# The first layer of a two-layer graph attention kernel: adjacency in four column quadrants, weights turned in 32x32 blocks on VectorE, and masks and low halves on GpSimd

## The reference

```
h = relu(layernorm(x))
Wh1, Wh2 = (h @ W) @ a[:256], (h @ W) @ a[256:]
e = leaky_relu(Wh1 + Wh2.T, 0.2)
attention = softmax(where(adj > 0, e, -1e12), axis=1)
negative  = -softmax(where(adj > 0, -e, -1e12), axis=1)
x = x + elu(concatenate([attention @ h, negative @ h], axis=1) @ wtrans)
```

## Time and profile before

| | |
|---|---|
| median of 3 runs | 2782.67 us (2781.08 to 2784.18) |
| profiled execution, its own time | 2782.04 us |
| its span | 2780.3 us |
| first block, first instruction of l0b to first of g0 | 69.2 to 1099.9 us |
| PE busy | 2666.2 us, 96% |
| DVE busy | 2351.9 us, 85% |
| ACT busy | 1558.1 us, 56% |
| POOL busy | 1216.3 us, 44% |

### The profile page before, as it was taken

The page is one execution under the profiler, slowest core; times in us unless marked ns, Lnnn a source line. Parts: engine busy times, 40 slices in busy tenths (PEclk is TensorE's granted clock), DMA queues, the critical chain, the costliest instruction groups (busy, mean ns, idle before and its releaser), DMA issues. The chain is left out here.

```text
span 2780.3 us, 54929 instructions
## 1 busy us (share of the span) xinstructions
PE 2666.2 (96%) x20240; PEld 2550.2 (92%) x20240; DVE 2351.9 (85%) x3292; ACT 1558.1 (56%) x2419; POOL 1216.3 (44%) x706
## 2 busy tenths in 40 slices
PE   4799999999999997999999999997999999999997
PEld 2699999999999996899999999997899999999997
DVE  8898998888888894488888988888588888988888
ACT  5466666666666664555555555554455555555554
POOL 5444444544555440044444444445044454544446
PEclk8899999999999999999999999999999999999999
DMA  2222222222222221133333333333233333333333
GB/s 102 78 77 79 68 79 77 81 69 75 75 76 79 73 63 54 52 88 103 92 107 92 107 94 103 94 96 101 97 88 111 96 114 96 114 96 102 107 97 109
DMA packets 100926, 247.53 MB, mean 89 GB/s; under 512 B 9360, under 2 KB 51088, under 8 KB 100752
## 3 DMA queue, kind: packets, MB, share of 16 engines
q1 hardware_dynamic: 98880, 243.30, 29.5%
q10 hardware_dynamic: 1872, 1.84, 0.2%
HBM read 232.52 MB, written 12.58 MB: 88 GB/s over the span
## 5 line engine op out<-in xcount | busy, mean ns | idle before, releaser
L91 PE MATMUL l0b_acc<-l_h_parts,l0b_turned_hi 128*128 128x512 f32 x1984 | 759.0, 415 | 0.0
L485 POOL TENSOR_SCALAR l_adj_pieces<-l_adj_pieces 128x1024 f32<-128x1024 f32 x124 | 471.1, 3799 | 502.4 <-DMA l_adj_pieces<-in_adj_dram 502.4
L92 PE MATMUL l0b_acc<-l_h_parts,l0b_turned_lo 128*128 128x256 f32 x1984 | 556.4, 280 | 0.0
L503 ACT CAST l0b_turned_hi<-l0b_turn_psum 128x512 fp32r<-128x512 f32 x512 | 299.5, 586 | 336.2 <-PE l0b_turn_psum L668 332.1
L1066 POOL TENSOR_TENSOR g0b_sum_wide<-g0b_sum_wide,g0b_slab 128x512 f32<-128x512 f32 x240 | 311.4, 1298 | 396.2 <-DVE g0b_masked_psum L1174 386.1
L1066 POOL TENSOR_TENSOR g1b_sum_wide<-g1b_sum_wide,g1b_slab 128x512 f32<-128x512 f32 x240 | 316.0, 1317 | 339.2 <-DVE g1b_masked_psum L1174 328.4
L589 DVE TENSOR_TENSOR l0b_turned_lo<-l0b_turn_psum,l0b_turned_hi 128x512 fp32r<-128x512 f32 x512 | 351.8, 687 | 120.8 <-ACT l0b_turned_hi L503 118.2
L91 PEld LDWEIGHTS l0b_acc<-l_h_parts,l0b_turned_hi 128*128 128x128 f32 x1984 | 374.1, 189 | 66.3 <-issue 0.3
L92 PEld LDWEIGHTS l0b_acc<-l_h_parts,l0b_turned_lo 128*128 128x128 f32 x1984 | 374.9, 189 | 0.0
L80 PE MATMUL g0b_acc<-g_wh_parts,g0b_part_hi 128*128 128x256 f32 x1024 | 293.6, 287 | 6.8 <-DVE g0b_part_lo L1180 5.7
L80 PE MATMUL g1b_acc<-g_wh_parts,g1b_part_hi 128*128 128x256 f32 x1024 | 293.6, 287 | 5.7 <-DVE g1b_part_lo L1180 4.6
(11 more groups left out here) (219 smaller groups left out, 7317.0 us busy)
## 6 DMA issues: line engine op xcount, KB each, us to landing
g_adj_ring<-in_adj_blocks_dram SPq DMA_DIRECT2D x256, 512.0 KB, 3.7
l_adj_pieces<-in_adj_dram SPq DMA_DIRECT2D x128, 512.0 KB, 3.8
l0b_x_in<-in_x_dram SPq DMA_DIRECT2D x32, 128.0 KB, 3.1
x_rows<-l0b_x SPq DMA_DIRECT2D x32, 128.0 KB, 3.0
g0a_rows<-x_rows SPq DMA_DIRECT2D x8, 512.0 KB, 4.7
g0b_y<-x_rows SPq DMA_DIRECT2D x16, 256.0 KB, 4.1
v_rows<-g0b_y SPq DMA_DIRECT2D x16, 256.0 KB, 4.5
g1a_rows<-v_rows SPq DMA_DIRECT2D x8, 512.0 KB, 5.2
```

The lines of the kernel that those rows point to most:

```text
L91: pe.matmul(out, lhs_hi, rhs, start=first, stop=False)
L92: return pe.matmul(out[:, width:], lhs_lo, rhs[:, :width], start=False, stop=False)
L485: pool.tensor_scalar(adj_pieces[:, q, :], adj_pieces[:, q, :], 0.0, PENALTY, ALU.is_le, ALU.mult).then_inc(penalty_ready, 1)
L503: act.copy(turned_hi[:, s % RING, :], turn_psum[:, s % RING, :]).then_inc(hi_ready, 1)
```

## The change

Another layout of adj, another engine for four of the operations, and another order of work.

- The host cuts adj into blocks of 32 rows, and each into column quadrants: block f is a [128, 1024] tile whose partition (q, r) holds row r of the block, and of every 128 columns the 32 of quadrant q. A tile of 128 rows is four such blocks a. `r_quad` and `s_quad` hold r and s in that layout, both divided by 2^60; ACT writes the former in four small pieces per group in l0a, and l0a ends with a spread of s over the quadrants (four small matmuls) and some small tables (`own`, `fold`).
- Penalties are adj - 1 on POOL, a `tensor_tensor` subtract of a broadcast 1.0 (L535), in place of `tensor_scalar` (L251 and L485). l0a makes none.
- The score is one ACT instruction, Prelu with bias s, from `r_quad` to PSUM (L559), in place of DVE's L567. The masked scores are still DVE's, with the factor 2^60 in them (L632), and now read the score from PSUM.
- In this layout turning the 32 x 32 blocks where they stand gives the turned weights, so that DVE's `transpose` of 1024 columns, SBUF to SBUF (L657), takes the place of the 64 TensorE turns per tile. It reads four row blocks at once, so it waits for four exponentials of its sign.
- `split` on ACT (L574) now works on 1024 columns from SBUF. `rest`, the low half, moves from DVE and PSUM to POOL and SBUF (L541), 8 per tile with 1024 columns.
- A row's maximum and sum now lie in four partitions: `turn_max`, `join_max`, `spread_max`, `take_max` for the maximum and `spread_sum`, `totals` for the sum join them through small TensorE and DVE operations.
- The order is one list of steps n, unrolled, eight to a tile: masks at n, exponentials 9 steps behind, turns 13, split and rest 14, weighing 16. The rings hold three entries, and the score two.

The diff's core (the counterparts of `mean_rows`, `project_means` and elu only change their indices):

```diff
-                    for q in range(PIECES):
-                        pool.wait_ge(adj_in[q], 16)
-                        pool.tensor_scalar(adj_pieces[:, q, :], adj_pieces[:, q, :], 0.0, PENALTY,
-                                           ALU.is_le, ALU.mult).then_inc(penalty_ready, 1)
...
                     def take_r(g):
                         act.wait_ge(r_ready, g + 1)
-                        act.copy(r_row[:, g * BANK:(g + 1) * BANK], r_psum[:, g % 2, :]).then_inc(r_copied, 1)
+                        by_quad = r_psum[:, g % 2, :].rearrange("p (b q c) -> p q b c", q=4, c=QUAD)
+                        for q in range(4):
+                            here = slice(q * QUAD, (q + 1) * QUAD)
+                            last = act.mul(r_quad[here, g * P:(g + 1) * P].rearrange("p (b c) -> p b c", c=QUAD),
+                                           by_quad[here, q, :, :], 1.0 / FAR)
+                        last.then_inc(r_copied, 1)
...
+                    for a in range(4):
+                        last = pe.matmul(s_psum[:, a * T:(a + 1) * T], spots[:, a, :, :].rearrange("p q r -> p (q r)"),
+                                         s_high[:], start=True, stop=True)
+                    last.then_inc(s_spread, 1)
...
+            POS_RING, NEG_RING = 2, 3
+            TURN_RING = 3
+            PART_RING = 3
+            SLOTS = 8
+            FRONTS = T * SLOTS
+            TO_EXP, TO_TURN, TO_SPLIT, TO_WEIGH = SLOTS + 1, SLOTS + 5, SLOTS + 6, 2 * SLOTS
...
+                    for n in range(STEPS):
+                        f, rest = divmod(n - 1, 2)
+                        if rest == 0 and 0 <= f and f + ADJ_SLOTS < T * 4:
+                            sp.wait_ge(masked, 2 * f + 2)
+                            fetch_adj(sp, f + ADJ_SLOTS)
...
-                    with pool.Fori(32, 16 * T + 16, 16) as arrived:
-                        for q in range(PIECES):
-                            pool.wait_ge(adj_in[q], 16)
-                            pool.wait_ge(adj_in[q], arrived)
-                            pool.tensor_scalar(adj_pieces[:, q, :], adj_pieces[:, q, :], 0.0, PENALTY,
-                                               ALU.is_le, ALU.mult).then_inc(penalty_ready, 1)
+                    def penalty(f):
+                        slot = adj_ring[:, f % ADJ_SLOTS, :]
+                        pool.wait_ge(adj_in[f % ADJ_SLOTS], 16 * (f // ADJ_SLOTS + 1))
+                        pool.tensor_tensor(slot, slot, unit[:].to_broadcast([P, PIECE]), ALU.subtract
+                                           ).then_inc(penalty_ready, 1)
+
+                    def rest(m):
+                        pool.wait_ge(hi_ready, m + 1)
+                        wait(pool, products, m - PART_RING + 1)
+                        pool.tensor_tensor(turned_lo[:, m % PART_RING, :, :], turned[:, m % TURN_RING, :, :],
+                                           turned_hi[:, m % PART_RING, :, :].bitcast(F32), ALU.subtract
+                                           ).then_inc(lo_ready, 1)
+
+                    pool.memset(max_parts[:], 0.0).then_inc(padded, 1)
+                    penalty(0)
+                    for n in range(STEPS):
+                        f, odd = divmod(n, 2)
+                        if odd == 0 and f + 1 < T * 4:
+                            penalty(f + 1)
+                        if 0 <= n - TO_SPLIT < FRONTS:
+                            rest(n - TO_SPLIT)
...
+                    def score(f):
+                        t, a = divmod(f, 4)
+                        wait(act, masked, 2 * (f - 1))
+                        act.activation(score_psum[:, f % 2, :], r_quad[:], ACT.Prelu, bias=s_quad[:, a, t:t + 1],
+                                       alpha=SLOPE_0).then_inc(score_ready, 1)
...
+                    def split(m):
+                        act.wait_ge(turns, m + 1)
+                        wait(act, products, m - PART_RING + 1)
+                        act.copy(turned_hi[:, m % PART_RING, :, :], turned[:, m % TURN_RING, :, :]
+                                 ).then_inc(hi_ready, 1)
...
+                    for n in range(STEPS):
+                        if 0 <= n - TO_SPLIT < FRONTS:
+                            split(n - TO_SPLIT)
+                        if 0 <= n - TO_EXP < FRONTS:
+                            exponential(n - TO_EXP)
+                        f, odd = divmod(n, 2)
+                        if odd == 0 and f + 1 < T * 4:
+                            score(f + 1)
...
-                            dve.scalar_tensor_tensor(
-                                out=score[:], in0=r_row[:, cols], scalar=s_high[:, bass.ds(t, 1)],
-                                in1=r_row_low[:, cols], op0=ALU.add, op1=ALU.max).then_inc(score_ready, 1)
...
-                        n = G2 * t + s
-                        dve.wait_ge(hi_ready, n + 1)
-                        dve.tensor_tensor(turned_lo[:, s % RING, :], turn_psum[:, s % RING, :],
-                                          turned_hi[:, s % RING, :].bitcast(F32), ALU.subtract
-                                          ).then_inc(lo_ready, 1)
...
+                        t, a, sign = front(f)
+                        tau = 4 * t + a
+                        dve.wait_ge(score_ready, tau + 1)
+                        dve.wait_ge(penalty_ready, tau + 1)
+                        if f == 0:
+                            dve.wait_ge(padded, 1)
+                        if a == 0 and sign == 0:
+                            wait(dve, max_turned, t - 1)
+                        ring = POS_RING if sign == 0 else NEG_RING
+                        if t >= ring:
+                            dve.wait_ge(turns, SLOTS * (t - ring) + 4 * (sign + 1))
+                        dve.tensor_tensor_reduce(part(t, sign)[:, a, :], adj_ring[:, tau % ADJ_SLOTS, :],
+                                                 score_psum[:, tau % 2, :], FAR, LOWEST,
+                                                 ALU.add if sign == 0 else ALU.subtract, ALU.max,
+                                                 max_parts[:, t % 2, 2 * a + sign:2 * a + sign + 1]
+                                                 ).then_inc(masked, 1)
...
+                    def join_max(t):
+
+                        dve.wait_ge(max_turned, t + 1)
+                        wait(dve, max_spread, t)
+                        folded = max_psum.rearrange("p (o q r) -> p o r q", o=1, r=QUAD)
+                        dve.tensor_reduce(max_joined[:], folded.to_broadcast([P, 4, QUAD, 4]), AX, ALU.max,
+                                          negate=True).then_inc(max_join, 1)
...
+                    def take_max(t):
+                        dve.wait_ge(max_spread, t + 1)
+                        wait(dve, exp_ready, SLOTS * (t - 1))
+                        dve.tensor_copy(neg_max[:, t % 2, :, :].rearrange("p a s -> p (a s)"), spread_psum
+                                        ).then_inc(neg_max_ready, 1)
...
+                    def turn(m):
+                        t, sign, k = back(m)
+                        dve.wait_ge(exp_ready, SLOTS * t + 4 * (sign + 1))
+                        wait(dve, lo_ready, m - TURN_RING + 1)
+                        cols = part(t, sign)[:, :, k * TILES * QUAD:(k + 1) * TILES * QUAD]
+                        dve.transpose(turned[:, m % TURN_RING, :, :].rearrange("p b (a r) -> p a b r", r=QUAD),
+                                      cols.rearrange("p a (b c) -> p a b c", c=QUAD)).then_inc(turns, 1)
...
+                    for n in range(STEPS):
+                        if 0 <= n - TO_TURN < FRONTS:
+                            turn(n - TO_TURN)
+                        joining = group_at(n, JOIN)
+                        if joining is not None:
+                            join_max(joining)
+                        if n < FRONTS:
+                            masked_part(n)
+                        if joining is not None:
+                            take_max(joining)
...
-                        for k in range(TURNS):
-                            col = g * BANK + k * P
-                            last = pe.transpose(turn_psum[:, s % RING, k * P:(k + 1) * P], rows[:, col:col + P],
-                                                ident)
-                        last.then_inc(turns, 1)
...
+                    def turn_max(t):
+                        pe.wait_ge(masked, SLOTS * (t + 1))
+                        wait(pe, elu_ready, t - 2)
+                        pe.transpose(max_psum, max_parts[:, t % 2, :], ident).then_inc(max_turned, 1)
+
+                    def spread_max(t):
+                        pe.wait_ge(max_join, t + 1)
+                        pe.matmul(spread_psum, max_joined[:].rearrange("p q r -> p (q r)"), ident[:, 0:8], start=True, stop=True).then_inc(max_spread, 1)
...
+                    def weigh(m, k):
+                        t, sign, c = back(m)
+                        if k == 0:
+                            pe.wait_ge(lo_ready, m + 1)
```

(16 more changed lines are left out.)

378 lines of the change are left out of this document (168 added, 210 removed).

## The result

| | before | after |
|---|---|---|
| median of four executions | 2781.88 us (2780.25 to 2784.18) | 2698.69 us (2695.62 to 2704.45) |
| ratio | | 0.9703, 95% interval 0.9685 to 0.9721 |
| profiled execution, its span | 2782.04, 2780.3 us | 2695.62, 2693.8 us |
| transfer that opens g0 | 1099.88 us | 1011.74 us |

The change takes 83 us off by the medians, 86.4 by the two profiled executions, and 2696 had been predicted. The transfer that opens g0 comes 88.1 us earlier; the two other layers give about 1.7 back. But inside the first layer two terms were wrong by more than 50 us each, with opposite signs.

The account below looks back on a forecast made before the run. GpSimd was taken as the bound at 29.1 us a tile: 64 + 24 + 904 + 5 + 5 + 2.9 + 8.9 = 1014 us against 1099.9, so 2782.0 - 86 = 2696 us, range 2640 to 2800.

Parts of the forecast that it names:

- The turns are free of the port, 1.22 us: DVE's block transposes in the loop: 1.22 us per 1024-column turn, 9.8 us a tile, not excluded by GpSimd.
- The largest rival: DVE's turns exclude GpSimd at the shared port: 2800 to 2990 us, middle 2870; 15 in 100 together with slow turns.
- Low halves at 2.41: GpSimd's eight low-half instructions of 1024 columns in a tile: 2.41 us each from start to start.
- Penalties at 2.41: GpSimd's four penalties in a tile: 2.41 us each; with the low halves 12 x 2.41 = 28.9 us a tile.
- The quick rival: GpSimd's broadcast subtract costs about a one-input cast, other engines bound at 25 to 26 us: 2590 us; 7 in 100.
- L691 waits at most 2.4 us, and both circles have 4 us to spare: Second elu step on DVE: up to 2.4 us wait per tile; GpSimd's and TensorE's loops: over 4 us spare.
- Nothing charged for the clock: TensorE in the loop: stands still about 0.7 us in each 3.6, 84% busy, clock at 1.00, no time added.
- GpSimd near 100% and a tile of 29.1: First layer's loop: GpSimd nearly 100% busy as the bound, a tile of 29.1 us.
- the prediction's own signs of error: Wrong if L657 shows two durations or over 1.9 us, L535 differs from L541, or GpSimd idles until ACT or PE.
- TensorE at 24.5: TensorE per tile: 31.0 us less 7.0 for the turns, plus 0.5 for small operations, 24.5 us.
- ACT and DVE: Time per tile in the loop: ACT 23.2 us; DVE 22 us, with hand-overs 23 to 24.
- The ends: First layer around the steady loop: l0a from 69 to 64 us, fill 24, last steps 5, weighing 2.9, tail 8.9.

Follow-up runs that it names:

- run 3: The changed kernel with the penalty's 1.0 read from a row of 32 ones repeated, instead of one repeated element: 2752.3 us, ratio 0.9899.
- run 6: run 1 with the penalty's 1.0 read from a row of 32 ones repeated, instead of one repeated element: 2685.56 us, ratio 0.9654.
- run 1: The changed kernel with the first elu step writing back to PSUM, so L691 has one SBUF and one PSUM input: 2628.63 us, ratio 0.9447.
- 10: run 1 plus an idle DVE instruction reading PSUM alone, 3.36 us at the elu's place in each tile: 2696.27 us, ratio 0.9694.
- 12: run 1 plus an idle DVE instruction reading PSUM alone, 3.35 us at step 1 in each tile: 2627.84 us, ratio 0.9446.
- run 7: run 1 with the penalty taken on only 32 of the 1024 columns, the others keeping raw adjacency: 2583.63 us, ratio 0.9288.
- run 9: run 1 with two of the four penalties a tile on DVE instead of GpSimd, 1.0 as an immediate: 2608.31 us, ratio 0.9377.
- run 4: The changed kernel with a second copy of L691 added, its result thrown away: 2659.44 us, ratio 0.9559.

## Why the prediction came out right, by its steps

- **The turns are free of the port, 1.22 us**: right, 1.24 (L657), its maximum beside its minimum. The largest rival had that as its condition. **Low halves at 2.41**: right (2.42, start to start 2.38). The small gap between neighbours that the prediction took over from L251 isn't there: they overlap.
- **Penalties at 2.41**: mis-sized. 1.90, or 1.85 from start to start, in the changed kernel. By durations that is 4 x 0.55 = 2.2 us a tile, 68 us over 31 tiles, in the kernel's favour; by runs it is 54 to 57 us, since at the assumed price too the instructions start closer together than 2.41 (run 3 against the changed kernel, run 6 against run 1). The quick rival had the cause half right (a broadcast is cheap) and the size too low (1.04, a one-input cast of 1024 columns in l0a).
- **L691 waits at most 2.4 us, and both circles have 4 us to spare**: this step failed, in size and in kind. L691 takes 3.66 us in the mean of 150 to 950 and up to 6.8. And the circle that it stands in was not among those worked out: L691, the last masks, `turn_max` in TensorE's order, weighing and the turned means, ACT's L586, DVE's L680, and L691 again, 24.06 us and L691 itself. Its members are read from the waits; what runs 1, 10 and 12 together show is the price of the place: without the wait -70 us; an equal delay without any port +68, the lower clock of some tiles included; the same delay at step 1, 0. In step 1 it hides in the waits that DVE has anyway. With the penalties at the price that was assumed, the waits cost 67 us (run 3 against run 6).
- **Nothing charged for the clock**: wrong. The idle time was taken as 0.7 us in each 3.6; TensorE instead stood still for up to 4.7 us at a stretch, and came back at 0.50. Eleven tiles by 2.1 us are about 23 us, worked out from tile lengths, not by a run of its own.
- **GpSimd near 100% and a tile of 29.1**: it was 93% and 28.7 (27 tiles from 171.64 to 945.73). About 2 us of each were idle, and GpSimd's own work is the 26.4 of run 1. Of the prediction's own signs of error two appeared: L535 differs from L541, and GpSimd's idle time ends with ACT.
- **TensorE at 24.5**: 24.96 with no idle time (run 7), as far as that run can tell it. **ACT and DVE**: in run 1 they have 426.5 and 404.0 of 480 us, 23.5 and 22.2 a tile, for 23.2 and 22 plus hand-overs.
- **The ends**: l0b starts at 67.1 (64), the first low half is at 90.0 (88), the last one ends at 996.7 (1002), and the tail takes 15.0 us (11.8), its projections 0.41 us each at a granted clock of 0.72. The step to g0 at 1011.7 for 1014.

So the outline (TensorE loses its turns, GpSimd has the most to do) was right, and GpSimd is indeed the bound where L691's wait is taken away (runs 1 and 6). In the changed kernel itself the length of a tile follows that wait. The closeness of 2698.7 to 2696 is luck: run 6, with the assumed price and no wait, takes 2685.6 and opens g0 at 1000.7 where the sum had 1014; the waits add 67 to that (run 3, 2752.3, above the 2675 to 2740 that the forecast gave by itself), and the cheap penalties take 54 off.

How L691's wait comes to be 1.3, 2.5 or 6.8 us, that is, which end of a GpSimd instruction lets it in, stays open. Where it began about 1.4 us into a low half, it was let in at that one's end, 12 times of 12. Where it began 0.1 to 0.2 us into one, it was let in at its end 5 times (626.34 is one) and 12 times only when GpSimd had run out of work (568.12). The one-input instruction of run 9, begun as early in a low half, was let in at its end every time. That run 4 settled where the changed kernel did not is shown, but its cause is not.

## What to carry to other kernels

Before moving work to GpSimd, list the DVE instructions with two SBUF inputs or at the fast copy rate, and ask for each what stands behind it in a loop of engines, not how long it is: here 0.42 us once in 28 decided 70. An input in PSUM in place of one of the two freed it here (run 1). An engine's slack is not one number: 3.35 us on VectorE cost nothing at one step and 68 us at another, so a ring that is worked out for the stream says nothing about a small reduction that TensorE waits for in order. And a prediction that hits should be checked term by term.
